# A cross-attention and mixture-of-experts kernel: VectorE's small dependent operations issued in turns

## The reference

```python
# attention block (q = layernorm(x), k = v = context)
ig, fg = gi @ igate_w.T + igate_b, gi @ fgate_w.T + fgate_b      # gate logits, gi = [q, k, v]
cs = cumsum(log_sigmoid(fg))
log_D = where(causal, cs[:, None] - cs[None, :], -inf) + ig[None, :]
m = max(log_D, -1)
C = (q @ k.T / sqrt(dh)) * exp(log_D - m)
h = C / (max(abs(C.sum(-1)), exp(-m)) + 1e-6) @ v
x1 = x + (h - h.mean(-1)) / sqrt(h.var(-1) + 1e-5) * out_w       # per head of 32 features
# expert block
xf = layernorm(x1)
s = softmax(xf @ gate_w);  top2, idx = top_k(s, 2);  top2 /= top2.sum()
y = sum over the two chosen experts of top2 * (gelu(xf @ w1 + b1) @ w2 + b2)
out = x1 + y
```

## Time and profile before

| | |
|---|---|
| runs | 648.76, 648.89 and 652.68 us, median 648.89 |
| the profiled execution | 651.1 us, of which the span of the trace is 649.1 us |
| mean granted TensorE clock | 0.986 |
| busy share of the span | PE 94%, PE weight load 81%, VectorE 75%, ScalarE 50%, GpSimd 30% |

### The profile page before, as it was taken

One profiled execution on the slowest core, in us unless ns is written; L12 is line 12 of the kernel. 1 busy time (PEld: TensorE's weight loads), 2 busy tenths in 40 slices (PEclk: granted clock), 3 DMA queues, 4 the chain that ended last, 5 costly groups with the idle time before them and its releaser, 6 DMA issues. The chain is left out here.

```text
span 649.1 us, 20273 instructions
## 1 busy us (share of the span) xinstructions
PE 611.4 (94%) x6736; PEld 526.6 (81%) x6737; DVE 487.2 (75%) x1330; ACT 323.4 (50%) x767; POOL 193.7 (30%) x185
## 2 busy tenths in 40 slices
PE   1799999999999899999999999999999999999995
PEld 1567777777777668998988988888989888989994
DVE  2546988999999898995888967666676757575684
ACT  2677888897988747544432323233232323232341
POOL 3000002242433424235345523232222323232333
PEclk9898998999999999999999999999999999999998
DMA  4443635475655626233464432323132323243510
GB/s 143 134 127 118 209 99 187 147 238 194 220 166 142 198 91 231 70 73 92 75 186 108 70 68 38 65 36 65 33 62 33 66 33 66 67 119 81 141 34 2
DMA packets 56044, 70.22 MB, mean 108 GB/s; under 512 B 5584, under 2 KB 50832, under 8 KB 55840
## 3 DMA queue, kind: packets, MB, share of 16 engines
q1 hardware_dynamic: 42560, 51.80, 26.3%
q0 software_dynamic: 13296, 17.32, 14.7%
q10 hardware_dynamic: 112, 0.08, 0.0%
HBM read 41.50 MB, written 24.92 MB: 102 GB/s over the span
## 5 line engine op out<-in xcount | busy, mean ns | idle before, releaser
L1059 ACT ACTIVATE decay_slots<-scores,b_turned 128x256 f32<-128x256 f32 (+1 forms) x312 | 124.4, 451 | 241.2 <-PE scores L1545 235.1
L1545 PE MATMUL scores<-x_slots,w_halves 128*128 128x256 f16 (+1 forms) x1760 | 193.7, 266 | 0.0
L1545 PEld LDWEIGHTS scores<-x_slots,w_halves 128*128 x1760 | 165.2, 98 | 17.3
L662 POOL DMA_INDIRECT expert_rows<-xf_rows,slot_i x64 | 71.9, 1124 | 211.8 <-issue 107.0
L1559 PE MATMUL pv<-w_halves,decay_slots 128*128 x864 | 97.6, 273 | 0.0
L684 POOL DMA_INDIRECT out_rows<-v_centred_and_one,row_ids x36 | 58.3, 1619 | 129.2 <-DVE v_centred_and_one L2146 95.7
L1559 PE MATMUL gate_bank<-w_halves,q_and_k_halves 128*128 x840 | 95.0, 273 | 0.0
L1559 PEld LDWEIGHTS pv<-w_halves,decay_slots 128*128 128x128 f16 x864 | 84.4, 98 | 9.7
L1559 PEld LDWEIGHTS gate_bank<-w_halves,q_and_k_halves 128*128 128x128 f16 x840 | 82.0, 98 | 9.5
L684 POOL DMA_INDIRECT out_rows<-work,row_ids x35 | 56.2, 1605 | 104.6 <-DVE work L2146 82.6
L1278 PEld LDWEIGHTS pv<-v_centred_and_one,decay_slots 128*128 128x128 f32 x512 | 63.7, 194 | 1.6
(11 more groups left out here) (263 smaller groups left out, 864.5 us busy)
## 6 DMA issues: line engine op xcount, KB each, us to landing
weight_stage<-in_L_ffn_w SPq DMA_DIRECT2D x32, 512.0 KB, 4.0
x_slots<-in_x SPq DMA_DIRECT2D x16, 512.0 KB, 4.4
weight_stage<-expert_rows SPq DMA_DIRECT2D x30, 272.0 KB, 3.2
ctx_slots<-in_ctx SPq DMA_DIRECT2D x8, 512.0 KB, 6.0
out_rows<-x_slots SPq DMA_DIRECT2D x8, 512.0 KB
v_centred_and_one<-expert_rows SPq DMA_DIRECT2D x9, 272.0 KB, 3.0
expert_rows<-v_centred_and_one SPq DMA_DIRECT2D x9, 272.0 KB, 3.2
xf_rows<-w_halves SPq DMA_DIRECT2D x4, 512.0 KB, 4.1
```

Source lines behind the costliest of these rows:

```text
L662: pool.indirect_dma_start(table, bass.IndirectOffsetOnAxis(ap=sloti[:, step[1], j, k:k + 1], axis=0), xfn[:, step[1], j, :], None, bounds_ ...
L1059: ins = act.activation(hf[:, f * R:f * R + tr.rows(0)], ps_s[:, q, n * R:n * R + tr.rows(0)], ACT.Gelu, bias=b1T[:, bass.ds(expert, 1), f] ...
L1545: ins = pe.matmul(o, w, xh[:, tr.slot(0) % 2, b, k, 0:tr.rows(0)], start=(n == 0), stop=(n == 3 * KC - 1))
```

## The change

VectorE's functions become generators that stop (`yield`) after each operation whose result the next one needs, and the wait for it moves to the resumption. `body` then calls `go_on` to issue one piece of a chain at a time, with pieces of other chains or large operations between. The operations, their number, their operands and their waits stay as they are; the lists of PE, ACT, GpSimd and the DMA queues keep their orders. `whole` runs a chain through, in the first steps and in the tail. Inside `h_norm` the 128x1024 sum of squares moves behind the four normalizer operations; inside `records` the addition to the ranks moves up to the second place. The diff, cut to its core:

```diff
+                def go_on(chain):
+                    next(chain, None)
+                def whole(chain):
+                    for _ in chain:
+                        pass
                 def refine(c, var, y, t):
-                    c.link(dve, dve.tensor_tensor(t, y, y, ALU.mult))
...
+                    c.inc(dve.tensor_tensor(t, y, y, ALU.mult))
+                    yield
+                    c.wait(dve)
...
                 def h_norm(step):
...
+                    rows = Hs[:, :, :, DH]
+                    c.inc(dve.scalar_tensor_tensor(out=nrm[:, :, :], in0=rows, scalar=-1.0, in1=rows,
+                                                   op0=ALU.mult, op1=ALU.max))
+                    yield
+                    c.wait(dve)
...
+                    c.inc(dve.scalar_tensor_tensor(out=hv[:, :], in0=n, scalar=LN_EPS, in1=n,
+                                                   op0=ALU.mult, op1=ALU.mult))
+                    yield
                     sq = work[:, :, :].rearrange("p j (h e) -> p (j h) e", h=NH)
                     c.inc(dve.tensor_reduce(ssq[:, :], sq, AX, ALU.add))
-                    rows = Hs[:, :, :, DH]
...
+                    yield
+                    c.wait(dve)
                     dve.scalar_tensor_tensor(out=hv[:, :], in0=ssq[:, :], scalar=1.0 / DH, in1=hv[:, :],
...
                     dve.wait_ge(s_lg, g + 1)
-                    c.link(dve, dve.tensor_reduce(m1[:, :], ps_log, AX, ALU.max))
-                    c.link(dve, dve.tensor_tensor(dl[:, :, :], ps_log, wide(m1[:, :]), ALU.subtract))
...
+                    c.inc(dve.tensor_reduce(m1[:, :], ps_log, AX, ALU.max))
+                    yield
+                    c.wait(dve)
+                    c.inc(dve.tensor_tensor(dl[:, :, :], ps_log, wide(m1[:, :]), ALU.subtract))
+                    yield
+                    c.wait(dve)
...
                 def body(last, step, nxt, after):
...
-                    if step is not None:
-                        h_norm(step)
-                    if nxt is not None:
-                        weights_low(nxt, 2)
-                    if step is not None:
-                        h_scaled(step)
-                        h_weighted(step)
-                    if last is not None:
-                        choose(last)
-                    if after is not None:
-                        gate_bias(after)
+                    for _ in range(5):
+                        go_on(norm)
+                    if nxt is not None:
+                        weights_low(nxt, 2)
+                    go_on(norm)
+                    go_on(choice)
+                    go_on(choice)
+                    go_on(scaled)
+                    go_on(choice)
...
+                    go_on(scaled)
+                    go_on(choice)
+                    if step is not None:
+                        h_weighted(step)
+                    go_on(choice)
+                    go_on(bias)
+                    go_on(choice)
+                    go_on(bias)
+                    go_on(choice)
                     if nxt is not None:
                         c_of(nxt, 0)
+                    go_on(choice)
                     if after is not None:
                         log_f(after)
+                    go_on(choice)
                     if step is not None:
                         x1_of(step)
...
-                    if step is not None:
-                        x1_stats(step)
-                    if last is not None:
-                        records(last)
+                    for _ in range(SB + 1):
+                        go_on(outgoing)
+                    go_on(record)
+                    go_on(outgoing)
+                    go_on(record)
+                    go_on(record)
+                    go_on(record)
```

More of the change, by code:

```diff
@@ L1916, in body @@
                 def body(last, step, nxt, after):
+                    nothing = iter(())
+                    incoming, scaling = (next_stats(after), next_norm(after)) if after is not None else (nothing,) * 2
+                    sums, bias = (next_a(nxt) if nxt is not None else nothing,
+                                  gate_bias(after) if after is not None else nothing)
+                    parted = split(nxt) if nxt is not None else nothing
+                    norm, scaled = (h_norm(step), h_scaled(step)) if step is not None else (nothing,) * 2
+                    choice, record = (choose(last), records(last)) if last is not None else (nothing,) * 2
+                    outgoing = x1_stats(step) if step is not None else nothing
                     if last is not None:
@@ L1991, in first_steps @@
                     running_max(S1)
-                    split(S1)
+                    whole(split(S1))
                     weights_low(S1, 2)
                     max_log_decay(S1)
-                    h_norm(S0)
-                    h_scaled(S0)
+                    whole(h_norm(S0))
+                    whole(h_scaled(S0))
                     h_weighted(S0)
@@ L2182, in _ @@
                 split_rows(Turn(0, 0), 0)
-                h_norm(last)
+                whole(h_norm(last))
                 split_rows(Turn(0, 0), 1)
                 row_fields(Turn(0, 0), 1)
-                h_scaled(last)
+                whole(h_scaled(last))
                 h_weighted(last)
```

177 lines of the change are left out of this document (112 added, 65 removed).

## The result

| | before | changed |
|---|---|---|
| median, 17 runs each on the same chip | 651.13 us | 657.63 us |
| lowest and highest | 646.76, 653.97 | 652.02, 660.15 |
| profiled execution: span | 649.1 us | 656.9 us |
| its mean granted TensorE clock | 0.986 | 0.979 |

The ratio is 1.0104, with a 95% interval of 1.0077 to 1.0131: the changed kernel is about 6.5 us slower. The forecast was 4.9 us slower.

What follows compares the result with a forecast made beforehand. VectorE's list was taken to set the pace of a body. Four bodies (4.6 us), the fifth (0.5) and the first steps (-0.1) gave +4.9 us, forecast as a median of 653.8 us; own range 650.3 to 655.4, wider range 649.0 to 658.0.

Steps and rivals of the forecast that it cites:

- the last variance operation: In `h_norm` on VectorE, second body: starts at 144.86 and ends at 145.05, where before it ended at 144.03.
- the delay of the logits: ScalarE's logarithm waits for the late variance; its later copy and the logits move by 0.60 us, 1.02 in the fifth body.
- The end of the body: From first aggregation to next body: earlier reciprocal wins 0.18 us, two shrunken pauses 0.12, together 0.30 us per body.
- The fifth body: Last body, without gate bias or `log_f`: logits delayed by 1.02 us, 0.30 won at the end; grows by 0.5 us.
- a rival of the first statement alone: Small operations cost the same in turns, 0.224 us each: 3.5 us more a body, 666 us in all; chance 0.02.
- the clock's rival: TensorE's clock falls at further pauses: one to four bodies 1.6 us longer, 655.4 to 660.2, taken at 657; chance 0.10.
- the sum at full clock: Four bodies 4.6 us longer, the fifth 0.5, `records` in the first steps 0.1 shorter: +4.9 us in all.
- within 1%: Outcome of the whole kernel's time within 6.5 us of no change, given 0.74; slower was given 0.20.

Runs made afterwards that it cites:

- experiment 2: Changed kernel with `choose` moved behind the refinements and both multiplications, weight split behind the whole `h_norm`, turns kept: 648.24 us, ratio 0.9969 to the kernel before.
- experiment 4: Experiment 2 with the last variance operation put behind the weight split again, `choose` still late: 652.84 us, ratio 1.0060 to the kernel before.
- experiment 10: Changed kernel with the last variance operation right behind its reduction, ahead of the weight split, `choose` still early: 653.04 us, ratio 1.0060 to the kernel before.
- experiment 3: Changed kernel with only the turns of `records` at the end of the body kept, everything ahead whole in the old order: 651.36 us, ratio 1.0007.
- experiment 6: Kernel before with four more filler matmuls on TensorE ahead of `times_v(step,2)` in all bodies: 649.99 us, ratio 1.0004 to the kernel before.
- experiment 7: Experiment 2 with four more filler matmuls on TensorE ahead of `times_v(step,2)` in all bodies: 646.95 us, ratio 0.9940 to the kernel before.
- filler experiments: Four more filler matmuls in the changed kernel, the kernel before and experiment 2, or none in the changed kernel: ratios 1.0079, 1.0004, 0.9940, 1.0161.
- experiment 9: Experiment 2 with four more filler matmuls in bodies 1 to 4 alone: 644.79 us against 648.15 for the kernel before, ratio 0.9943.

## Why the prediction was right, and what it left out

**The place and the mechanism held.** VectorE arrives early at `choose`, stands for the logits, and the refinements and large multiplications that used to fill this time stand behind. Forecast: about 3.1 us idle in bodies 1 to 4 and 2 in the fifth. Measured: 2.83 and 1.86 at full clock. Experiments 2, 4 and 10 show it as a cause: with both undone the loss turns into a gain, with the early wait alone undone nothing of it is left (27.35 against 27.40), and with the late variance alone undone half of it goes. One reading in the prediction is wrong and changes nothing: what ends 2.5 us after VectorE gets to `choose` is the logits (147.44 or 147.47 against 144.97), not ScalarE's copies, of which the last ends at 146.49.

**The steps of an undisturbed body**, from its start, forecast and measured: the last variance operation at 13.40 and 13.40; `choose` at 16.61 and 16.42; from there to `x1_of` 5.47 and 5.42; from `x1_of` to the next body 6.45 and 6.37. The body was to grow by 1.14 and grew by 0.82. Most of the difference is in the second step, the delay of the logits, sized at 0.60 and measured at 0.40. ScalarE's copy did move by 0.54. But in the kernel before the first matmul started 0.15 us behind its weight load (146.54 and 146.69 in the earlier trace rows), and now it starts with it: that little slack took part of the delay. I had moved the end of the matmuls by as much as the copy. The end of the body gained 0.37 alone (experiment 3) and was sized at 0.30. The fifth body was to grow by 0.5 and grew by 0.31.

**What small operations cost.** The prediction took 0.11 us for an operation in another chain's gap, by rows of the kernel before, and the rows after show just that. The Trainium skill's page "VectorE: DVE Perf Modes", section "The DRAIN you can't avoid", has the next operation wait until the pipeline of the one before is empty, but adds that an operation which is not held starts earlier; the prediction made a rival of the first statement alone. The trace disagrees with that one for operations in turns (0.11 against 0.22), as do the shorter bodies of experiments 2 and 3; it fits the addition, though no run here tests which operations the skill counts as held.

**The term that was left out of the sum.** At full clock the change costs 4 x 0.82 + 0.31, about 3.6 us. The medians differ by 6.5. The rest goes with TensorE's clock: 22.7 us at half clock against 16.1, and 6.6 x 0.38 to 0.48 is 2.5 to 3.2 us (an estimate, since the 16.1 come from another set of runs). The prediction had this as a rival with a chance of 0.10, at 1.6 us for a body with a fall. The prediction looked for the pauses that the change adds, ahead of the logits and at `c_of(nxt,0)`; the falls came right behind the pause at L1142, which the kernel before has too. Both size and chance were too low: I took the price from one fall of 3.5 us, and here a fall lasted 10 us and cost the fourth body 4.2 (32.41 against 28.22). It was not a rival to the forecast either but a companion of it. In the profiled executions the end of the loop moved from 243.67 to 251.17, 7.50 us: the bodies' differences are 3.59, 0.82, 0.82, 5.01 and 0.31, and the first began 3.05 earlier. In the first steps the kernel before had more time at half clock: its granted clock was 0.89 from 20 to 50 us and 0.94 from 50 to 80 us, in the changed kernel it was 0.94 and 1.00. That this makes up the 3.05 is likely and not shown.

That the total lies in the range is thus in part luck: the sum at full clock was 1.3 us too large, and the clock, which was not in it, added about 3. The median of 657.63 lies above the forecast's own range (650.3 to 655.4), where the prediction had put the clock's rival; 2.2 us of the distance to 653.8 come from the kernel before, which was itself slower in the runs beside the change (651.13 against 648.89). By the chances given, the result at 1.04% lies just over the line between "within 1%" and "slower".

**What stays open.** The pause at L1142 is as long in the changed kernel as before (1.04 us), and yet the changed kernel is at half clock for longer. In its second body TensorE has a little more idle time (busy 26.49 of 28.21 us against 25.88 of 27.39, so 1.72 idle against 1.51), and the filler experiments show that idle time taken out at L1142 lowers the time at half clock; which of the pauses decides in a given body they don't show. Nor is the late gather of experiments 6 and 7 explained.

## What to carry to other kernels

Before an operation that waits for another engine is moved forward in an in-order list, compare when this engine gets there with when the result is there, and then look back: if anything that stands behind or just ahead of it feeds the engine it waits for, the wait grows by its own delay. Turns are worth having where the chain's inputs are long there, as at the end of the body here (0.37 us of each), and are to be filled with work that doesn't wait. And in a stage where TensorE has pauses of a microsecond, price the clock with the longest fall that the trace shows, not with the one at hand: 0.89 over the 30 us from 20 to 50 us in the kernel before is 6.6 us at half clock, nearly twice the fall that was priced, and still short of the 10 us that came. The best version measured has the later `choose` and four filler matmuls in bodies 1 to 4 (3.4 us under the kernel before in experiment 9; 1.4 without the filler in experiment 2, with intervals that overlap). Filler in all five bodies gained nothing for the kernel before; in bodies 1 to 4 alone it was not tried there.

## What was not expected of the hardware

Pauses of the same 1.04 us were followed by 10 us at a granted clock of 0.50 in the fourth body and by a clock of 1.00 in the two bodies before it, in one execution of one kernel; with 1.69 us the time at half clock rose to 37.4 us on average, and with 0.19 us it fell to 15.9. Over four sets of runs a microsecond at half clock cost 0.38 to 0.48 us.
